# Sum of squares by transposes and VectorE sums, and the input gate's second pass put ahead of the up product's transposes

## What is computed

```
xn    = layernorm(x)                                # [16, 512, 256]
up    = xn @ up_w.T                                 # 512 wide
gate  = xn @ gate_w.T
shift = silu(conv4(up) + conv_b)
v     = sigmoid(up @ ig_w1.T @ ig_w2.T + ig_b2) * up          # "input gate"
q, k, g, tau = projections of shift;  o = chunked scan(q, k, v, g, tau)
xg    = (o + shift * residual_weight) * silu(gate)
rms   = rsqrt(mean(xg * xg, over the 512 features) + 1e-5)    # "sum of squares"
out   = x + (xg * rms * norm_weight) @ down_w.T + ffn(xn)
```

## Time and profile before

| | us |
|---|---|
| median of 3 runs | 1940.59 (1940.5 to 1941.85) |
| the profiled execution | 1940.21 |
| its span on the core | 1938.4 |
| TensorE busy | 1921.8 |
| VectorE busy | 1584.1 |
| ScalarE busy | 1295.3 |
| GpSimd busy | 81.2 |

### The profile page before, as it was taken

How to read it: one execution, slowest core, us unless ns; L and a number is a source line. 1 busy time by engine, 2 the same in 40 slices (tenths; PEclk the granted TensorE clock), 3 DMA queues, 4 the chain that set the end, 5 groups by cost and what they waited for, 6 DMA issues and landing times.

```text
span 1938.4 us, 46120 instructions
## 1 busy us (share of the span) xinstructions
PE 1921.8 (99%) x16804; PEld 1902.9 (98%) x16804; DVE 1584.1 (82%) x4304; ACT 1295.3 (67%) x2687; POOL 81.2 (4%) x136
## 2 busy tenths in 40 slices
PE   8999999999999999999999999999999999999998
PEld 7999999999999999999999999999999999999998
DVE  7788888888788887888888788787888878888887
ACT  5666667767676766666766667675667666667575
POOL 0000000000000000000000000000000000000000
PEclk9999999999999999999999999999999999999999
DMA  8000000000000000000000000000000000000000
GB/s 309 7 12 13 12 2 12 12 12 12 13 1 12 13 12 12 8 5 13 12 13 12 7 6 12 13 12 13 1 12 13 12 12 12 1 13 12 13 7 8
DMA packets 23538, 34.19 MB, mean 18 GB/s; under 512 B 3170, under 2 KB 19810, under 8 KB 23364
## 3 DMA queue, kind: packets, MB, share of 16 engines
q1 hardware_dynamic: 23364, 31.43, 4.8%
HBM read 23.04 MB, written 8.39 MB: 16 GB/s over the span
## 4 chain that ended last, share of the span: by engine, by line
PE 94%; issue 2%; ACT 1%; DVE 1%; SPq 1%; DMA 0%; POOLq 0%; POOL 0%; DVEq 0%; ACTq 0%
PE fb L383 64%; PE ab L383 21%; PE ab L593 2%; PE ab L628 1%; PE ab L529 1%; PE ab L453 1%; PE ab L518 1%; PE ab L583 1%; PE fb L678 1%; SPq L289 0%; PE ab L590 0%; PE ab L469 0%; PE ab L606 0%; ACT wwhole L726 0%; DMA sgate<-stage_w 0%
## 5 line engine op out<-in xcount | busy, mean ns | idle before, releaser
L383 PE MATMUL fb<-hid1h,wwhole 128*128 128x256 f32 x2048 | 474.2, 279 | 0.1
L383 PE MATMUL fb<-hid1l,wwhole 128*128 128x256 f32 x2048 | 467.9, 276 | 0.0
L383 PE MATMUL fb<-hid0l,wwhole 128*128 128x256 f32 x2048 | 465.9, 276 | 0.0
L383 PE MATMUL fb<-hid0h,wwhole 128*128 128x256 f32 x2048 | 465.8, 276 | 0.0
L383 PEld LDWEIGHTS fb<-hid1h,wwhole 128*128 128x128 f32 x2048 | 384.5, 188 | 4.0 <-ACT raw L838 0.3
L383 PEld LDWEIGHTS fb<-hid1l,wwhole 128*128 128x128 f32 x2048 | 384.7, 188 | 0.0
L383 PEld LDWEIGHTS fb<-hid0h,wwhole 128*128 128x128 f32 x2048 | 384.5, 188 | 0.0
L383 PEld LDWEIGHTS fb<-hid0l,wwhole 128*128 128x128 f32 x2048 | 384.4, 188 | 0.0
L838 ACT ACTIVATE raw<-fb,sh_s 128x256 f32<-128x256 f32 x512 | 212.3, 465 | 150.3 <-PE fb L383 142.7
L383 PE MATMUL fb<-xntl,wwhole 128*128 128x256 f32 x1024 | 237.5, 276 | 0.0
L383 PE MATMUL fb<-xnth,wwhole 128*128 128x256 f32 x1024 | 237.5, 276 | 0.0
(11 more groups left out here) (234 smaller groups left out, 4481.6 us busy)
## 6 DMA issues: line engine op xcount, KB each, us to landing
xin<-x SPq DMA_DIRECT2D x32, 256.0 KB, 2.7
out<-xin SPq DMA_DIRECT2D x32, 256.0 KB, 2.2
stage_more<-stage_w SPq DMA_DIRECT2D x6, 512.0 KB, 7.1
sgate<-stage_w SPq DMA_DIRECT2D x4, 512.0 KB, 4.4
shift<-stage_w SPq DMA_DIRECT2D x4, 512.0 KB, 5.0
v<-stage_w SPq DMA_DIRECT2D x4, 512.0 KB, 5.6
raw<-stage_w SPq DMA_DIRECT2D x3, 512.0 KB, 6.0
mixed<-stage_w SPq DMA_DIRECT2D x3, 512.0 KB, 8.2
```

The costliest lines, as they stand in the source:

```text
L383: mm = pe.matmul(o, a, b, start=start and i == 0, stop=stop and i == len(pairs) - 1)
```

## The change

Two parts. `input_gate(1)` stands ahead of the eight transposes. And the sum of squares is made by other operations: ScalarE squares in two pieces, VectorE adds blocks 0 and 1, blocks 2 and 3, and then both sums (three additions in place of one reduction); TensorE transposes `sqsum` twice, 128 by 128, in place of the two matmuls with a column of ones; and VectorE sums the transposed squares out of PSUM into `total`, waits for that, and makes `msq` from it.

```diff
@@ sq_d, sqsum_d, total_d
-        sq_d, xg_hi, ln_hi = sig("sq_d", 1), sig("xg_hi", 1), sig("ln_hi", 1, 1)
+        sq_d, xg_hi, ln_hi = sig("sq_d", 2), sig("xg_hi", 1), sig("ln_hi", 1, 1)
-        sqsum_d = sig("sqsum_d", 1)
+        sqsum_d, total_d = sig("sqsum_d", 4), sig("total_d", 1)
@@ TensorE
                     layer1(m)
+                input_gate(1)
 
                 for c in range(NC):
                     pe.wait_ge(x_ev.sem, x_ev.at(me))
                     for d in range(DB):
                         mm = pe.transpose(ab[c][:, d * P:(d + 1) * P], xbuf[:, d, W - 1 + c * CH:W - 1 + (c + 1) * CH], ident_s[:])
                     mm.then_inc(xt_mm.sem, 1)
-                input_gate(1)
@@ TensorE, end of the half
                 for c in range(NC):
-                    mm = pe.matmul(fb[1][:, c:c + 1], sqsum[:, c * CH:(c + 1) * CH], ones[:, 0:1], start=True, stop=True)
+                    mm = pe.transpose(fb[1][:, c * P:(c + 1) * P], sqsum[:, c * CH:(c + 1) * CH], ident_s[:])
@@ ScalarE
-                act.activation(sq[:], sgate[:], ACT.Square).then_inc(sq_d.sem, 1)
+                for d in (0, 2):
+                    act.activation(sq[:, d:d + 2, :], sgate[:, d:d + 2, :], ACT.Square).then_inc(sq_d.sem, 1)
@@ VectorE
-                dve.wait_ge(sq_d.sem, sq_d.at(me))
-                dve.tensor_reduce(sqsum, sq.rearrange("p d t -> p t d"), mybir.AxisListType.X, ALU.add).then_inc(sqsum_d.sem, 1)
+                for d in (0, 2):
+                    dve.wait_ge(sq_d.sem, sq_d.at(me, d // 2 + 1))
+                    dve.tensor_tensor(sq[:, d, :], sq[:, d, :], sq[:, d + 1, :], ALU.add).then_inc(sqsum_d.sem, 1)
+                dve.wait_ge(sqsum_d.sem, sqsum_d.at(me, 2))
+                dve.tensor_tensor(sqsum, sq[:, 0, :], sq[:, 2, :], ALU.add).then_inc(sqsum_d.sem, 2)
@@ VectorE, end of the half
                 dve.wait_ge(rs_mm.sem, rs_mm.at(me))
-                dve.tensor_scalar(msq[:], fb[1][:, 0:NC], 1.0 / DI, EPS, ALU.mult, ALU.add).then_inc(msq_d.sem, 1)
+                dve.tensor_reduce(total[:], fb[1][:, 0:NC * P].rearrange("p (c k) -> p c k", c=NC), mybir.AxisListType.X,
+                                  ALU.add).then_inc(total_d.sem, 1)
+                dve.wait_ge(total_d.sem, total_d.at(me))
+                dve.tensor_scalar(msq[:], total[:], 1.0 / DI, EPS, ALU.mult, ALU.add).then_inc(msq_d.sem, 1)
```

More of the change, by code:

```diff
@@ L184, in layer_program @@
         ssk, rkn = sb("ssk", [P, NC]), sb("rkn", [P, NC])
-        msq, rms = sb("msq", [P, NC]), sb("rms", [P, NC])
+        msq, rms, total = sb("msq", [P, NC]), sb("rms", [P, NC]), sb("total", [P, NC])
         later_k, earlier_q = sb("later_k", [P, 1]), sb("earlier_q", [P, 1])
```

## The result

| | before | after |
|---|---|---|
| median (range) of 8 runs each, us | 1940.26 (1939.0 to 1941.85) | 1947.38 (1945.02 to 1949.76) |
| the profiled execution, us | 1940.21 | 1947.89 |
| its span, us | 1938.4 | 1946.1 |

A forecast was written before the change was run, and what follows sets the result against it. TensorE was taken as the bound, busy 1921.8 of 1938.4 us. Terms: 7.1 - 4.3 + 0.1 + 0.3 = +3.2 us on the median 1940.59, some 1943.8, stated as 1943.5; range 1938.0 to 1946.5.

The forecast's parts named there:

- the wait: Moved input gate: L518 waits for ScalarE's L767, 0.27 us at place 0, 0.19 at place 1, 7.1 us in all.
- the transposes: Sum of squares on TensorE: two transposes replace four records, saving 0.14 us per half (bounds 0.09 and 0.15), 4.3 us.
- the order: Swapping the order of matmul types around the transposes and L518 costs about 0; 0.1 us put for all halves.
- the tail: Last half's end, uncovered: TensorE 0.14 us sooner, VectorE 0.46 later, so it grows by 0.3 us.
- rival B: Loop's back edge loses cover: up to 0.14 us at 15 edges, up to 2.1 us more, 1945.6; chance 0.22.
- Rivals A and D: A: L518's wait is covered, 1936.7, chance 0.12. D: its exposed load isn't paid, 7.1 becomes 3.7, 1940.1, chance 0.11.
- the signs that I named: Among them: L518 waiting for L767 some 31 times, 0.15 to 0.3 us each; TensorE idle 3 to 7 us larger.
- Rival C: Sum of squares on TensorE: the transposes save nothing, the 4.3 us are missing, 1947.8; chance 0.05.
- VectorE and the covers: VectorE saves 0.76 us, loses 0.42 and about 0.04 per half; the next convolution stays covered, so 0 us.

The follow-up runs named there:

- sum_mid: As sum_only, but the two transposes stand between the two halves of the down product; 1948.28 us, ratio 1.0039 to the kernel before.
- sum_unroll: As sum_only, with three sequences in the loop's body, so 4 jumps back and not 14; 1951.19 us, ratio 1.0041 to the kernel before.
- after_again: The changed kernel word for word once more, a single run; 1949.63 us.
- half_dve: The changed kernel with input_gate(1) between the first four and last four transposes, plus one small VectorE instruction per half; 1944.50 us, ratio 1.0012 to before.
- gate_early: The changed kernel with ScalarE's second gate eviction (L767) put ahead of the convolution's silu; 1944.72 us, ratio 1.0017 to the kernel before.
- early_levels: As gate_early, with the six small level matmuls in the order 0, 1, 2 and not 2, 1, 0; 1938.88 us, ratio 0.9979 to before.
- sum_only: The changed kernel with input_gate(1) back behind the transposes, so the new sum of squares alone; 1943.62 us, ratio 1.0017 to the kernel before.
- sum_levels: As sum_only, with the six small level matmuls in the order 0, 1, 2; 1954.88 us, ratio 1.0064 to the kernel before.

## Why the prediction was wrong

The step that failed is the sum: +3.2 us out of the wait, the transposes, the order and the tail, with nothing for the pace of TensorE's unchanged streams (measured +3.7), nothing for the code behind the loop (+1.4), and nothing for the back edges, which stood beside it as rival B (+2.0). The terms that it did have came out nearly as worked out.

**The wait of L518: right.** I had 0.27 and 0.19 us per half, 7.1 in all; measured are 0.25 and 0.18 (at a place 1 the two distances around L518 are 0.19 and 0.34, each against 0.11 and 0.23), 6.9 in all. The working by the earlier trace rows held, the 0.06 of the release and the 0.11 of the exposed load too, but not their places: L518 starts with its load, 0.05 us behind L767 and not 0.17, and the 0.11 shows behind it. Rivals A and D are out. Two details were wrong. In the first half I let the wait cost nothing by the earlier trace rows; there TensorE was late only through before's half clock, and in after it costs 0.25 us there too. And of the signs that I named, the list of waits has 15 and not some 31, and TensorE's idle time grew by 2.5 us, not by 3 to 7: at a place 0 the record of the matmul ahead lasts to 1127.32, over the start of L518 at 1127.30, so TensorE never counts as idle there.

**The transposes: right in the ordinary case.** 0.147 us per half end against 0.14, 4.6 us in all. Rival C is out, though its 1947.8 lies nearer to the measured time than the forecast does; that is luck. Two slips in the working changed nothing: 0.36 - 0.22 is 0.14, so the lower bound was 0.11 and not 0.09; and the 0.36 us of the four records is 0.09 each, so it doesn't quite fit the 0.107 that I held against it.

**VectorE and the covers: right.** The new reduction (L1257 of the changed kernel) takes 424 ns (I took 420), and VectorE's busy time fell by 15 us (I had 11) without any effect. The next half's convolution still waits for ScalarE at both places (against the earlier trace rows):

```profile
1057.83 0.98 DVE L1005 SCALAR_TENSOR_TENSOR shift<-xbuf,convw_s,shift 128x256 f32<-128x256 f32 x2 [0.57 <-ACT shift L741]
...
1117.12 0.98 DVE L1005 SCALAR_TENSOR_TENSOR shift<-xbuf,convw_s,shift 128x256 f32<-128x256 f32 x2 [1.32 <-ACT shift L741]
```

**The back edge (rival B): it came, and was larger per edge than I let it be.** I had 0.14 us of lost cover at up to 15 edges. In after 8 of the 14 edges stand out, by 0.2 to 0.5 us each, 2.0 us more than before in all; that this is near B's 2.1 in total is luck. I had set B against the forecast as its rival, though both can hold together. And the mechanism, cover by TensorE's last records, was wrong: sum_mid shows the loss with twelve long matmuls ahead. The Trainium skill ("Runtime: NRT & Kernel Launch", section "Instruction fetch mechanics") says that branching breaks the sequential prefetch: a taken branch to a target outside the instruction pages at hand holds execution until that page is fetched. The place of the waits agrees, the exit of sum_unroll among them (1.89 us); that sum_unroll's four jumps cost nothing and that the list with the four one-column records shows less of it, it doesn't explain.

**The wide pitch: missing.** 3.7 us of the 7.7 between the two spans, and no rival of mine had a place for it. I took 0.113 us per matmul as a property of the engine, because before's 64 streams all had it. Its trace could have warned me: the last 88 matmuls of its last half run at 0.118, at a granted clock of 1.00, as they do in all 20 profiles. Two of their starts, 86 matmuls apart:

```profile
1922.28 0.28 PE L383 MATMUL fb<-hid1l,wwhole 128*128 128x256 f32 x1
...
1932.41 0.28 PE L383 MATMUL ab<-wlo,parth 128*128 128x256 f32 x1
```

Every kernel with another TensorE list had some wide streams, between 1 and 31 of 64. This one term is enough to put the time out of the range: 1943.5 + 3.7 is 1947.2. What its size is in another execution isn't fixed: 3.7 us in after, 5.3 in after_again.

**The last sequence: missing, 1.4 us.** Its code stands outside of the loop. VectorE stands there 2.2 us for nothing that the profile names, and TensorE's small matmuls later wait for VectorE:

```profile
1847.79 0.29 DVE L1074 TENSOR_TENSOR small<-small 128x128 f32<-128x128 f32 x1 [2.23 <-issue]
```
```profile
1854.67 0.60 PE L590 MATMUL ab<-small 64*128 64x192 f32 x4 [0.73 <-DVE work L1123]
```

The same instruction so waits in nearly all kernels with VectorE's new list (2.1 to 2.4 us), and in none with the old one. It is absent in half_dve, with one VectorE instruction more per half, and in sum_unroll, with a longer loop. That fits a wait that hangs on where the instructions lie, and a fetch of them; both are argued, not shown.

**The tail: right up to the output.** I had +0.3 us. From the last down matmul to VectorE's last instruction it is 0.35 longer, as worked out. Behind it the transfer of the output and the end took 0.6 us less in after's profiled execution, so that the whole came out at -0.2; in nearly all of the 20 profiles that last part lies between 2.8 and 3.9 us, whatever the kernel.

## What to carry to other kernels

An instruction that moves past others takes its wait along: compare the end of its releaser with the time at which its weight load (not its matmul) is due in the new place, and add the load that no matmul covers. Here that gave 7.1 us, and 6.9 were measured. Where an engine is at 99%, look at the distance of the starts in its long streams too, before and after: a small edit far from a stream can change its pitch by 4% without any wait in the profile, and a range for such an edit must hold some us for it (0 to 14 us in these 20 profiles). And price a new list of instructions in its whole, the loop's jump and the code behind the loop among it.

## What the runs showed that I had not expected

- A stream of 128x256 float32r matmuls, each with its own weight load, has two steady pitches at the full granted clock, 0.113 and 0.118 us. It keeps one to its end, and in some kernels h2 had the pitch of its half's projection stream each time. The Trainium skill ("TensorE: Matmul & The Clock Gate", section "Back-to-back issue gap") has one figure for 256 columns, the gap of an isolated matmul: 262 cycles, or 0.109 us. None of these streams runs at that.
- Exchanging two of three pairs of small matmuls, equal in work, moved a kernel by some -7 us (gate_early to early_levels, by the ratios) or by +9 (sum_only to sum_levels).
- At a loop's jump TensorE lost up to 0.75 us with twelve long matmuls ahead of it (sum_mid), and at its exit once 1.8 us (sum_unroll).
- A weight load follows 0.05 us behind the end of the ScalarE activation that releases it, and when it is exposed, its 0.11 us shows between the first matmul and the next (0.34 us in after, 0.23 in gate_early), not ahead of the first.
